# Recommender tower with a compressed interaction network: load order of the first units, the last layer 1 in SBUF, the tower's first products ahead of the last sum, and the output in column order

## What is computed

```python
e = stack([tbl_f[ids[:, f]] for f in range(32)], axis=1)      # 1024 x 32 x 16, float32
xk = x0 = e
for W in (W0, W1, W2):                                        # 32 x 32 x 64, then 32 x 64 x 64 twice
    xk = relu(einsum('bmd,bhd,mhk->bkd', x0, xk, W))
    outs.append(sum(xk, axis=2))
h = concatenate([concatenate(outs, axis=1), dense_ctx], axis=1)   # 1024 x (3*64 + 16)
h = maximum(h @ W_top1 + b_top1, 0)                           # 208 -> 512
h = maximum(h @ W_top2 + b_top2, 0)                           # 512 -> 256
y = h @ W_top3                                                # 256 -> 1
```

## Time and profile before

| | |
|---|---|
| median of 3 runs | 638.2 us (636.67 to 640.62) |
| the profiled execution, its own time | 641.88 us |
| its span | 640.0 us |
| PE busy, share of the span | 575.2 us, 90% |
| DVE busy | 547.4 us, 86% |
| ACT busy | 465.8 us, 73% |
| POOL busy | 457.8 us, 72% |
| DMA | 153.16 MB, 239 GB/s over the span |

### The profile page before, as it was taken

One profiled execution on the slowest core, in us unless ns is written; L12 is line 12 of the kernel. 1 busy time (PEld: TensorE's weight loads), 2 busy tenths in 40 slices (PEclk: granted clock), 3 DMA queues, 4 the chain that ended last, 5 costly groups with the idle time before them and its releaser, 6 DMA issues.

```text
span 640.0 us, 9853 instructions
## 1 busy us (share of the span) xinstructions
PE 575.2 (90%) x2620; PEld 194.1 (30%) x2620; DVE 547.4 (86%) x298; ACT 465.8 (73%) x3336; POOL 457.8 (72%) x353
## 2 busy tenths in 40 slices
PE   0379779999999998999999999999998999989996
PEld 0144232323233233333232323232333433223332
DVE  0369896999999998999999999999999999999200
ACT  0226395979797979789797969696969689757422
POOL 6777676979797888888888989796988862434000
PEclk9989789999999998999999999999998999989999
DMA  3767793949585775849393939495776849333000
GB/s 96 238 221 262 279 424 101 414 167 370 216 333 233 280 307 219 367 164 415 123 418 125 419 130 408 169 374 201 283 293 233 352 173 407 129 136 91 1 0 0
DMA packets 29602, 153.16 MB, mean 239 GB/s; under 512 B 7487, under 2 KB 17579, under 8 KB 20971
## 3 DMA queue, kind: packets, MB, share of 16 engines
q1 hardware_dynamic: 14372, 144.32, 55.6%
q10 hardware_dynamic: 6983, 6.11, 3.1%
q0 software_dynamic: 8192, 2.11, 2.8%
HBM read 147.60 MB, written 4.92 MB: 238 GB/s over the span
## 4 chain that ended last, share of the span: by engine, by line
POOL 32%; PE 29%; issue 17%; DVE 10%; ACT 5%; DMA 5%; POOLq 0%; SPq 0%; ACTq 0%
PE acc L627 24%; POOL rows L398 20%; POOL prod_pool L411 12%; DVE prod L448 10%; ACT x L503 2%; PE x L700 2%; DMA rows<-table,ids_sb 2%; ACT relu_out L515 2%; DMA spread<-x_scratch 1%; PE x L689 1%; DMA spread<-x_scratch_half 1%; ACT x_pool L503 1%; PE x L706 1%; PE x L693 0%; PE acc L689 0%
## 5 line engine op out<-in xcount | busy, mean ns | idle before, releaser
L448 DVE TENSOR_TENSOR prod<-spread,x 128x2048 f32<-128x2048 f32 (+2 forms) x277 | 536.6, 2007 | 22.8 <-DMA spread<-x_scratch_half 11.1
L627 PE MATMUL acc<-prod,w 128*64 128x512 f32 (+1 forms) x2076 | 462.4, 582 | 56.2 <-DVE prod L448 42.8
L398 POOL DMA_INDIRECT rows<-table,ids_sb x256 | 242.8, 948 | 80.8 <-issue 75.8
L627 PEld LDWEIGHTS acc<-prod,w 128*64 128x64 f32 x2076 | 151.3, 140 | 350.7 <-issue 256.9
L411 POOL TENSOR_TENSOR prod_pool<-spread,x_pool 128x1024 f32<-128x1024 f32 (+1 forms) x93 | 214.8, 2344 | 51.6 <-ACT x_pool L503 51.2
L515 ACT ACTIVATE relu_out<-acc 128x16 f32<-128x16 f32 x992 | 166.3, 355 | 8.2 <-DVE xt L437 5.0
L515 ACT ACTIVATION_READ_ACCUMULATOR relu_out<-acc 128x1 f32 x992 | 166.9, 381 | 0.0
L503 ACT ACTIVATE x<-acc 64x512 f32<-64x512 f32 (+1 forms) x136 | 74.1, 545 | 100.7 <-PE acc L627 99.2
L523 ACT ACTIVATE relu_out<-relu_out 128x16 f32<-128x16 f32 x512 | 104.2, 410 | 0.0
L523 ACT ACTIVATION_READ_ACCUMULATOR relu_out<-relu_out 128x1 f32 x512 | 103.9, 395 | 0.0
L627 PE MATMUL acc<-prod_pool,w 128*64 128x512 f32 (+1 forms) x372 | 94.7, 586 | 0.3 <-POOL prod_pool L411 0.3
(11 more groups left out here) (24 smaller groups left out, 33.2 us busy)
## 6 DMA issues: line engine op xcount, KB each, us to landing
spread<-x_scratch SPq DMA_DIRECT2D x60, 2048.0 KB, 10.4
first<-x_scratch SPq DMA_DIRECT2D x15, 512.0 KB
spread<-x_scratch_half SPq DMA_DIRECT2D x7, 1024.0 KB, 9.3
rows<-table,ids_sb POOLq DMA_INDIRECT x256
x_scratch<-xt ACTq DMA_DIRECT2D x15, 256.0 KB
w<-w ACTq DMA_DIRECT2D x2, 512.0 KB, 5.1
spread<-x_scratch_half SPq DMA_DIRECT2D x4, 256.0 KB, 4.1
spread<-wt SPq DMA_DIRECT2D x2, 384.0 KB, 4.4
```

The source lines that it names most:

```text
L398: nc.gpsimd.indirect_dma_start(rows[u % 2][:, j * D:(j + 1) * D], None, table, bass.IndirectOffsetOnAxis(ap=index, axis=0)).then_inc(gathe ...
L448: nc.vector.tensor_tensor(prod[:, at:at + count, 0:n], tiles(u, t, count), x[:, 0:n].rearrange("p (a n) -> p a n", a=1).to_broadcast([P, c ...
L627: last = nc.tensor.matmul(parts(to[K * blk:K * blk + K, 0:n]), w, side(moving[:, 0:2 * n], blk), start=start, stop=stop)
```

## The change

Four edits. The loads of the first units are issued in another order (and DVE's transpose of unit 1 follows the first product of unit 0's layer 2). The bank of the last unit's layer 1 is copied to SBUF by ACT and summed from there, after the sums of layer 2 of the unit before. In the tower each block takes the sums of layers 1 and 2 and the dense input ahead of those of layer 3, each with a wait of its own; y of half 0 is made between the second matrix's products of half 1. y stands on partitions 0 and 32 and leaves as two rows, one DMA each, in the order of the columns; the order of samples is set on the host.

```diff
-            load_group(0, 1)
-            load_group(0, 2)
+            for g in range(1, GROUPS):
+                load_group(0, g)
             load_first(1)
-            load_group(0, 3)
...
-                if u + 2 < UNITS:
+                if 0 < u and u + 2 < UNITS:
                     load_first(u + 2)
...
                 load_group(u + 1, 3)
+                if u == 0:
+                    load_first(2)
...
             layer_1(0)
-            turn(1)
             for u in range(LAST):
                 dve.wait_ge(x_ready[0], u + 1)
                 for i in range(len(steps_of(2, u))):
+                    if i == 1 and u == 0:
+                        turn(1)
                     multiply(2, u, i, x1)
...
-                sum_kept(u, 0, src)
+                if u < LAST:
+                    sum_kept(u, 0, src)
+                else:
+
+                    act.wait_ge(summed[0], LAST)
+                    nc.scalar.activation(relu_out[0][:, :], src[:, :], ACT.Relu).then_inc(relu_1_last_ready, 1)
...
+            act.wait_ge(relu_1_last_ready, 1)
+            sum_from(LAST, 0)
             after_2(LAST)
...
-                if before:
+                if before == (1, LAST):
+                    pe.wait_ge(relu_1_last_ready, 1)
+                elif before:
...
+            for t in range(H1 // P):
+                for l in range(2):
+                    pe.wait_ge(summed[l], UNITS)
+                    sums_in(t, l)
+                dense_in(t)
+                pe.wait_ge(summed[2], UNITS)
+                sums_in(t, 2)
...
+                    if (t, g) == (0, 1):
+                        to_layer_3(0)
+            to_layer_3(1)
...
-            sp.wait_ge(y_out, 2)
             for g in range(2):
...
+                sp.wait_ge(y_out, g + 1)
+                sp.dma_start(out[g:g + 1, :], y[M * g:M * g + 1, :]).then_inc(stored, 16)
+            sp.wait_ge(stored, 32)
```

More of the change, by code:

```diff
@@ L225, in build @@
         h_2 = room(1, H2 // P * 2 * BLK).rearrange("p (s g n) -> p s g n", g=2, n=BLK)
-        y = room(1, 2 * BLK)[0:1, :].rearrange("p (g n) -> p g n", n=BLK)
+        y = room(1, BLK)
         acc = [ps(f"acc{i}", [P, BLK]) for i in range(2)]
@@ L247, in build @@
         x_pool_ready = [sem(f"x{l + 1}_pool_ready") for l in range(2)]
-        relu_2_ready, relu_last_ready = sem("relu_2_ready"), sem("relu_last_ready")
+        relu_2_ready = sem("relu_2_ready")
+        relu_1_last_ready, relu_last_ready = sem("relu_1_last_ready"), sem("relu_last_ready")
         summed = [sem(f"summed{l}") for l in range(3)]
@@ L313, in to_y @@
         def to_y(g):
-            return x2[0:1, g * BLK:(g + 1) * BLK]
+            return x2[M * g:M * g + 1, g * BLK:(g + 1) * BLK]
         block = ctx.enter_context(nc.Block())
@@ L517, in sum_kept, with sum_from @@
                 last.then_inc(summed[layer], 1)
+            def sum_from(u, layer):
+                kept = relu_out[layer][:, 0:width(u) // 2].rearrange("p (c b e) -> p b c e", c=4, e=D // 4)
+                for b in range(samples(u)):
+                    last = nc.scalar.activation(kept[:, b, :, :], kept[:, b, :, :], ACT.Copy,
+                                                accum_out=z[:, layer, z_at(u) + b:z_at(u) + b + 1])
+                last.then_inc(summed[layer], 1)
             def sum_2(u):
                 act.wait_ge(relu_2_ready, u + 1)
[L521 to L525, removed]
+                sum_from(u, 1)
             def base_tile(u):
@@ L619, in _ @@
                 act.wait_ge(y_mm, g + 1)
-                nc.scalar.activation(y[:, g, :], to_y(g), ACT.Copy).then_inc(y_out, 1)
+                nc.scalar.activation(y[M * g:M * g + 1, :], to_y(g), ACT.Copy).then_inc(y_out, 1)
         @block.tensor
@@ L680, in _, with sums_in, dense_in, to_layer_3 @@
             layer(LAST, 3, order_of(3, LAST))
[L682 to L690, removed]
+            def sums_in(t, l):
+                for g in range(2):
+                    own = slice(64 * g, 64 * g + K)
+                    last = nc.tensor.matmul(to_h1(t, g), w_top1[own, l, t * P:(t + 1) * P], z[own, l, :],
+                                            start=l == 0, stop=l == 2)
+                    if l == 2:
+                        last.then_inc(h1_mm, 1)
+            def dense_in(t):
                 for g in range(2):
                     own = slice(64 * g, 64 * g + D)
-                    nc.tensor.matmul(to_h1(t, g), w_dense[own, t * P:(t + 1) * P], dense[own, :],
-                                     start=False, stop=True).then_inc(h1_mm, 1)
+                    nc.tensor.matmul(to_h1(t, g), w_dense[own, t * P:(t + 1) * P], dense[own, :], start=False, stop=False)
+            pe.wait_ge(tower_in, 112)
+            for t in range(H1 // P):
[5 more added lines that the diff above has]
+                sums_in(t, 2)
+            def to_layer_3(g):
+                for s in range(H2 // P):
+                    pe.wait_ge(h2_out, 2 * g + s + 1)
+                    last = nc.tensor.matmul(to_y(g), w_top3[:, s:s + 1], h_2[:, s, g, :],
+                                            start=s == 0, stop=s == H2 // P - 1)
+                last.then_inc(y_mm, 1)
             pe.wait_ge(small_in, 48)
@@ L753 @@
             give("wt3", inputs["W_top3"])]
-    out = nc.dram_tensor("y_out_dram", (B, 1), mybir.dt.float32, kind="ExternalOutput").ap()
+    out = nc.dram_tensor("y_out_dram", (2, COLS), mybir.dt.float32, kind="ExternalOutput").ap()
     build(nc, *args, out)
     r = run_bass_kernel_spmd(nc, [arrays], core_ids=[0])
-    return r.results[0]["y_out_dram"]
+    y = np.asarray(r.results[0]["y_out_dram"])
+    halves = y[:, 0:S // 2].reshape(2, HALVES, S // 4).transpose(1, 0, 2)
+    rest = y[:, S // 2:].reshape(2, -1, S // 2).transpose(1, 0, 2)
+    return np.concatenate([halves.reshape(S, 1), rest.reshape(B - S, 1)])
```

## The result

The changed kernel takes 632.93 us, the median of 9 runs (630.48 to 635.42), beside 638.72 for the kernel before (9 runs, 636.67 to 641.64): a ratio of 0.9908 with an interval of 0.9883 to 0.9932, or 5.8 us. That is above the range of the prediction. All ratios here are of fast runs; one run of the changed kernel, when it was run again (g1), was slow (643.24 us, granted clock 0.940) and is left out.

A forecast was written before the change was run, and what follows sets the result against it. Three engines (POOL, DVE, PE) were within a few per cent of each other in the middle, POOL slowest by a hair. Gains of 8.5 + 2.6 + 1.7 + 1.5 + 2.5 = 16.8 us from 638.2 gave 621.4 us, range 618 to 629.

The forecast's parts named there:

- The head: First units, up to about 106 us: new load order lets DVE and POOL run earlier, 8.5 us (bounds 4.2 and 9.74).
- the second order change: Unit 2's `first` behind unit 1's last group: unit 2's group 0 lands at 61.2 instead of 68.5, ending DVE's 3.13 us idle.
- The prediction's own sign of being wrong: In the new profile, POOL still waiting around 100 us would mean the head's gain is not 8.5 us.
- The first order change: Unit 0's last group right behind group 2, before unit 1's `first`: DVE's 4.18 us stall before 40.63 goes.
- rival (b): Head: queued third group delays unit 1's gathers and store by 3 us, POOL starts little earlier; 629 us, chance 0.09.
- the third group: SP's queue beside unit 1's gathers: one more queued load group costs a gather nothing; otherwise 2.3 us, head wins 6.
- The pause and the half clock: PE before the last unit's layer 2: 2.6 us wait for ACT's sums goes, plus 1.7 us of slow clock after it.
- the next limit: Last unit: DVE's products end at about 593 us, less than 2 us ahead of PE's end at 594.9.
- rival (c): Tail limited by DVE, or the clock falls all the same: gain 14 us, 624 us; chance 0.06.
- The tower: PE's 1.51 us wait at 600.66 is filled with the first two layers' products: 1.5 us (bounds 1.0 and 1.5).
- Output: End of the kernel: three of four output DMAs leave the end, the last issued in 0.63 to 0.99 us: 2.5 us less.
- The base: The 16.8 us were subtracted from the runs' median, 638.2 us, not from the profiled execution's 641.88 us.

The follow-up runs named there:

- g1: The changed kernel, unaltered, run again for a second trace of its head; ratio 0.9925 to the kernel before.
- g3: The changed kernel with unit 2's store alone issued by SP ahead of unit 1's last group; ratio 0.9855 to the kernel before.
- f1: The changed kernel with the stores of units 1 and 2 issued by SP ahead of the preceding unit's last group; ratio 0.9839 to the kernel before.
- f4: The changed kernel with both stores ahead, all y products at the end and four layer-3 steps ahead instead of three; 625.91 us, ratio 0.9779 to the kernel before.
- f3: The changed kernel with four instead of three last layer-3 product steps ahead of the last unit's layer 2; ratio 0.9878 to the kernel before.
- e4: The kernel before with the output edit alone: y on two column groups, one output DMA a half; ratio 0.9911.
- e1: The kernel before with the head edit alone: new load order, unit 1's transpose behind one product; ratio 0.9995.

## Why the prediction was wrong, point by point

**The head: 8.5 us forecast, 0 to 2 measured.** The step that failed is the second order change: "`first` of unit 2 now stands behind the last group of unit 1, which ... no longer waits for unit 2's store", by which unit 2's first group "is issued about 4 us earlier, at 52.4". The group no longer waits for the store, but the store waits for the group. It took 2.6 to 3.0 us from the second issue to `first` in the four traces of the old head and 5.8 to 6.1 in the five of the changed one, so unit 2's first group was issued at 54.3 to 58.0 us, no earlier than the 52.3 to 56.4 of the old head, and landed at 63 to 69, not at 61.2. I had taken the store's time from the old order, where only the end of one group was ahead of it, and gave the longer queue no price. g3, which undoes that alone, wins 3.4 us. With both stores ahead, f1 and f4 gain on the kernel before 4.3 and 4.6 us more than their rests explain, where the changed head alone gains about nothing, so the stores' waits are about 4.4 of the 8.5 us. The prediction's own sign of being wrong is there: GpSimd waits 2.79 us ahead of 102.65.

The first order change was right in kind: the stall at 36 us is gone in every trace of the changed head. But most of it stands one step later: DVE waits 1.65 to 4.80 us (mean 3.6) ahead of layer 1 of unit 1, where the old head had 2.62 to 4.18 (mean 3.3) ahead of unit 0's last products. The size was read off one execution in which it was at its largest, and so was the landing of unit 1's first group: the forecast moved it from 43.4 to 41.2 us, but it is 41.8 in the mean of the four old traces (40.4 to 43.4) and 41.7 in the five changed ones (39.7 to 43.4), read at the next load of SP, which waits for it. By the transpose of unit 2 the old head stands at 47.3 to 51.3 us in four traces (mean 49.4) and the changed one at 46.5 to 50.3 in five (mean 48.6): 0.8 us, not the 3.2 forecast. Unit 1's store, too, lands later with the third group queued, by less (3.1 to 4.2 us from its second issue to `first`, 2.5 to 4.0 with the old order). That is rival (b); it had a chance of 0.09 and the mechanism for one store, not for both. Its time of 629 is too low because the tail fell short as well.

By the rule on round-robin between queue rows that the prediction took from the Trainium skill (DMA: Bandwidth & Descriptors, Queues, rings and completion order), the third group would cost a gather nothing. The traces agree on the cost: with three groups queued unit 1's last gather landed 5.0 to 7.2 us after its issue (five traces), with two 5.2 to 6.8 (four, among them the 6.76 of the earlier trace rows). Taken as turns of single pieces, as the prediction took it, the rule does not hold for ACT's stores, whose packets stood still for 3 us behind SP's; there the measurement decides. In that section the Trainium skill gives a packet as typically some 9 to 17 descriptors. The 151 pieces that SP's queue moved from 47.6 to 51.0 us are about 9 for each of 16 engines, so such turns could be as long as the wait; whether these pieces are its descriptors no run shows.

**The pause and the half clock: 4.3 us forecast, 1.4 measured.** The pause is gone and the clock stays full, as forecast: the first 16 passes of layer 2 take 3.60 us instead of 5.35. Here another step failed: DVE, named as "the next limit" and passed over as "less than 2 us ahead", took the rest. DVE itself stood 2.5 us for the last unit's groups (1.0 before), which it releases only with its own steps of layer 3 and which take 8.55 us to land. From 554.30 to the tower PE needs 37.6 us, not 34.6. This is rival (c), as a part of the outcome. f3 moves one step ahead of the wait and gets 2.1 us of it back.

**The tower: 1.5 forecast, 1.1 measured.** PE's wait is gone; the price of 0.5 us for the parted products was set at nothing.

**Output: 2.5 forecast, 4.2 alone, 3.1 in place.** The last DMA, of one row, took 0.24 us to issue, where the forecast took 0.63 to 0.99 from the old forms. The forecast gave y "0"; on two column groups it is worth 1.1 us, and the third edit takes just that away.

**The sum.** The tail's 8.3 us are 5.9, the head's 8.5 are 0 to 2. The base was right: from the trace of before, an execution 3 us above the median, the same subtraction would have been off by that too. What it could not mend is that the terms of the head were read from that execution.

What stays open: some 4 us of the 8.5 that even f1 and f4 do not show, of which the size of the first stall is a part; the first order change's two halves (the group, and the transpose behind one product), which were not run apart; and why the same load with the same work queued ahead of it lands up to 2 us later in one execution than in another (unit 1's first group: 5.3 to 7.4 us in the five traces of the changed head). The kernel's spread of 5 us arises in that stretch: from the transpose of unit 5 to that of unit 16 all traces take 376.1 to 376.8 us.

## What to carry to other kernels

A short transfer on which the next loads depend goes ahead of the long one, not behind it; moving a load forward in one queue can move a store that is issued behind it back, even on another queue. When a stall is taken away in a stretch that is fed by loads, cost the chain to the next landing from rows with the new queue ahead of it, and from more than one execution, if the runs spread by as much as the gain. Cut traces at a point behind which all executions agree, and compare the two sides apart.

## What had not been expected of the hardware

Passes on two column groups with 128 rows run in pairs: the starts of the two halves' y passes in e4 lie 0.01 us apart although the program gives all four of one half first, and eight passes take 1.89 us where four take 1.88. A store's 327 packets stood for 3 us behind the groups of another queue, while 63 packets of the gathers moved at the change from one group to the next. The granted clock goes with the waits: over the first 120 us its mean is 1.00 in f1, which waits least there, 0.99 in g3, 0.97 in the kernel after and 0.94 before, in e1 and in g1; from 120 us on it is 0.99 in all of these.
